# A graph layer's tail: neighbour sums scaled by diagonal matrices on TensorE instead of per-row factors on ScalarE and VectorE

## The reference, cut to what matters

```python
agg = segment_sum(alpha[:, None] * z[edge_src], edge_dst)   # alpha = e_exp / denom[edge_dst]
h_new = h_s + agg                                           # h_s = xn @ W_self.T
h_new = where(deg[:, None] > 0, h_new, h)                   # h = xn; a node without edges keeps its row
h_new = relu(h_new)
x = x + (xn + h_new) + mix(xn)
y = layernorm(x)                                            # goes to the router and the experts
```

## Time and profile before

| | us |
|---|---|
| median of 3 executions | 2349.81 (2349.37 to 2350.4) |
| the profiled execution's own time | 2345.32 |
| its span, first to last instruction | 2343.3 |
| busy in the span: PE / DVE / ACT / POOL | 1930.4 / 1649.2 / 687.6 / 1465.6 |
| mean granted TensorE clock | 0.879 |

### The profile page before, as it was taken

One profiled execution on the slowest core, in us unless ns is written; L12 is line 12 of the kernel. 1 busy time (PEld: TensorE's weight loads), 2 busy tenths in 40 slices (PEclk: granted clock), 3 DMA queues, 4 the chain that ended last, 5 costly groups with the idle time before them and its releaser, 6 DMA issues.

```text
span 2343.3 us, 43283 instructions
## 1 busy us (share of the span) xinstructions
PE 1930.4 (82%) x11471; PEld 1505.6 (64%) x11471; DVE 1649.2 (70%) x4135; ACT 687.6 (29%) x2860; POOL 1465.6 (63%) x1188
## 2 busy tenths in 40 slices
PE   6999699678888888888888888888867778899991
PEld 5555688556666666666666656666644458788881
DVE  6997699977777767777666766776756656445564
ACT  2444688531111111111111111111102344444550
POOL 5000556677888888888888788888780153744366
PEclk9999555579899999998898988889998789999996
DMA  8887888544445544445544444445557754545464
GB/s 216 260 256 226 280 284 295 160 126 121 123 123 132 154 124 124 123 125 146 138 123 122 124 123 122 122 123 138 138 124 182 171 154 113 154 136 145 138 171 124
DMA packets 308206, 368.12 MB, mean 157 GB/s; under 512 B 118624, under 2 KB 261707, under 8 KB 304982
## 3 DMA queue, kind: packets, MB, share of 16 engines
q1 hardware_dynamic: 165292, 223.65, 32.0%
q0 software_dynamic: 135840, 136.92, 24.4%
q10 hardware_dynamic: 6975, 6.40, 0.9%
HBM read 279.68 MB, written 85.98 MB: 156 GB/s over the span
## 4 chain that ended last, share of the span: by engine, by line
PE 40%; issue 13%; DVE 11%; DMA 7%; DVEq 4%; POOL 3%; SPq 2%; ACT 1%; ACTq 0%; POOLq 0%
PE bank L677 39%; DMA wexp<-func_rows,a_src 5%; DVE acc L1823 4%; DVEq L1580 2%; POOL wexp L641 2%; DVE onehot L1810 1%; DMA g_all<-sorted_d 1%; SPq L369 1%; POOL g_all L664 1%; PE bank L1026 1%; DVE work L1596 1%; DVEq L1823 1%; DVE work L1599 1%; DMA work<-mix_rows 0%; PE bank L849 0%
## 5 line engine op out<-in xcount | busy, mean ns | idle before, releaser
L641 POOL DMA_INDIRECT wexp<-func_rows,a_src x850 | 1060.9, 1248 | 263.4 <-issue 193.7
L677 PE MATMUL bank<-wexp,onehot 125*125 125x257 f32 x1700 | 557.2, 432 | 215.6 <-DVE acc L1823 156.1
L1823 DVE TENSOR_TENSOR acc<-bank,acc 125x257 f32 x850 | 355.7, 419 | 381.0 <-PE bank L677 244.4
L677 PEld LDWEIGHTS bank<-wexp,onehot 125*125 125x125 f32 x1700 | 316.8, 206 | 391.9 <-issue 298.2
L1810 DVE TENSOR_SCALAR onehot<-iota_r,a_rel,a_hi 125x125 f32<-125x125 f32 x850 | 320.7, 380 | 0.1
L609 POOL TENSOR_TENSOR work<-iota_h,a_hi 125x500 f32<-125x500 f32 x85 | 109.2, 1286 | 246.9 <-PE bank L714 165.4
L677 PE MATMUL bank<-g_all 128*128 128x128 f32 x1840 | 230.0, 278 | 15.4 <-issue 6.1
L654 POOL DMA_INDIRECT sorted_d<-acc,work x100 | 122.4, 1224 | 180.9 <-DVE acc L1967 98.0
L677 PEld LDWEIGHTS bank<-g_all 128*128 128x128 f32 x1840 | 217.8, 194 | 19.0 <-ACT g_all L1301 7.4
L664 POOL DMA_INDIRECT g_all<-y_d,work x100 | 131.0, 1310 | 139.2 <-DVE g_all L2137 77.8
L677 PE MATMUL bank<-w_s,work 128*125 128x256 f32 x800 | 216.2, 419 | 0.0
(11 more groups left out here) (275 smaller groups left out, 2817.4 us busy)
## 6 DMA issues: line engine op xcount, KB each, us to landing
wexp<-lr_d SPq DMA_DIRECT2D x85, 625.0 KB
wexp<-in_attr SPq DMA_DIRECT2D x25, 896.0 KB
sorted_d<-spare SPq DMA_DIRECT2D x72, 256.0 KB, 4.8
g_all<-sorted_d SPq DMA_DIRECT2D x115, 128.0 KB
y_d<-g_all SPq DMA_DIRECT2D x115, 128.0 KB, 3.1
wexp<-func_rows,a_src POOLq DMA_INDIRECT x850, 4.0
work<-xn_rows SPq DMA_DIRECT2D x38, 224.0 KB
xnT_d<-work SPq DMA_DIRECT2D x25, 250.0 KB, 4.4
```

The source lines that it names most:

```text
L641: pool.indirect_dma_start(ring[:, z, 0:D], None, func_rows, bass.IndirectOffsetOnAxis(ap=a_src[:, n // CS, n % CS:n % CS + 1], axis=0)).th ...
L677: return pe.matmul(o, l, r, start=first, stop=last_, **kw)
L1823: v.tensor_tensor(to, bank[3 + z % 2][0:R, 0:D + 1], to, ALU.add).then_inc(s("summed"), 1)
```

## The change: diagonal matrices and four products

ScalarE no longer touches the self rows. For each group it writes four matrices of 125x125 into a new buffer `diag` (two buffers, in slots of `g_all` that hold expert outputs later): the identity with its rows scaled by `have` for either block, and by `rden` for either block. TensorE multiplies the self rows by the first and the accumulator by the second, per block, into the same PSUM region: four calls of 256 columns in place of two of 512. `xn` is no longer part of it. VectorE then adds `xn` to the PSUM result in one instruction of 125x512, in place of the two of 125x256. All four products now wait for the group's four diagonals; these wait for `rden` (semaphore `have` at 3) and for the buffer, not for the group's loads.

```diff
+        diag = [g_all[0:R, 11 + k].rearrange("p j n -> p (j n)")[:, 0:4 * R].rearrange("p (a n) -> p a n", a=4) for k in range(2)]
...
                 freed(pe, s("c_r"), 2 * (g - 1))
                 pe.wait_ge(s(f"group_in{k}"), 32 * GIN[k] + 96 * (g // CBUF + 1))
                 to = pr_(2 + 2 * (g % 2))
-                mm(to, ident[0:R, 0:R], c_xn[k], True, False)
-                pe.wait_ge(s("c_have"), 2 * g + 2)
-                mm(to, ident[0:R, 0:R], c_self[k], False, True).then_inc(s("c_gnn"), 1)
+                pe.wait_ge(s("c_have"), 4 * g + 4)
+                for j in range(2):
+                    mm(to[:, j], diag[g % 2][:, j], c_self[k][:, j], True, False)
+                    last = mm(to[:, j], diag[g % 2][:, 2 + j], accv[:, 2 * g + j, 0:D], False, True)
+                last.then_inc(s("c_gnn"), 1)
...
-            def have_self(g):
-                k = g % CBUF
-                act.wait_ge(s("have"), 1)
-                act.wait_ge(s(f"group_in{k}"), 32 * GIN[k] + 96 * (g // CBUF + 1))
-                for j in range(2):
-                    act.activation(c_self[k][:, j], c_self[k][:, j], ACT.Copy,
-                                   scale=have[:, 2 * g + j:2 * g + j + 1]).then_inc(s("c_have"), 1)
+            def diagonals(g):
+                act.wait_ge(s("have"), 3)
+                freed(act, s("c_gnn"), g - 1)
+                for a, to_ in enumerate((have, rden)):
+                    for j in range(2):
+                        act.activation(diag[g % 2][:, 2 * a + j], ident[0:R, 0:R], ACT.Copy,
+                                       scale=to_[:, 2 * g + j:2 * g + j + 1]).then_inc(s("c_have"), 1)
...
-            o.did(v.reciprocal(rden, rden))
+            v.reciprocal(rden, rden).then_inc(s("have"), 1)
             v.wait_ge(s("have"), 1)
 
             def rows(g):
 
                 k = g % 2
                 v.wait_ge(s("c_gnn"), g + 1)
-                if g == 0:
-                    o.settle()
-                for j in range(2):
-                    v.scalar_tensor_tensor(c_x1[k][:, j], accv[:, 2 * g + j, 0:D], rden[:, 2 * g + j:2 * g + j + 1],
-                                           pr_(2 + 2 * k)[:, j], ALU.mult, ALU.add).then_inc(s("c_r"), 1)
+                v.wait_ge(s(f"group_in{g % CBUF}"), 32 * GIN[g % CBUF] + 96 * (g // CBUF + 1))
+                v.tensor_tensor(c_x1[k], pr_(2 + 2 * k), c_xn[g % CBUF], ALU.add).then_inc(s("c_r"), 2)
                 v.wait_ge(s("c_r"), 2 * g + 2)
                 v.sem_inc(s("c_t"), 1)
-                v.wait_ge(s(f"group_in{g % CBUF}"), 32 * GIN[g % CBUF] + 96 * (g // CBUF + 1))
```

More of the change, by code:

```diff
@@ L1276, in _ @@
                 if i < GROUPS:
-                    have_self(i)
+                    diagonals(i)
                 if 0 <= i - 1 < GROUPS:
```

## The result

| | before | after |
|---|---|---|
| median of 10 runs each, us | 2345.06 (2334.15 to 2350.4) | 2354.36 (2346.56 to 2362.56) |
| profiled execution, its own time and span, us | 2345.32, 2343.3 | 2351.19, 2349.1 |
| mean granted TensorE clock | 0.879 | 0.883 |

The ratio is 1.0043, 95% interval 1.0026 to 1.006: about 10.1 us slower (6.1 to 14.1); the two medians are 9.3 apart. The forecast was +9.8 us, set on the three runs known then, whose median of 2349.81 is 4.75 above that of the ten; so 2359.6 is 5.2 above what was measured, and the difference is nearly that of the forecast. By the same shift of the base 2354.36 lies just under the 2355 to 2367 that the forecast gave for itself. How much of that is luck, the stage has to show.

What follows compares the result with a forecast made beforehand. DMA was taken to bound groups up to 1847 us, a ring of waits (4.265 us a turn) those from 1860. Ring, routing and end terms of 7.8 plus 2.0 at the start gave +9.8, 2359.6 us, range 2353.5 to 2368.

Steps and rivals of the forecast that it cites:

- The ring that is late next: Diagonals, products, transposes, router, router_relu, next diagonals in one iteration: 4.91 us a turn, overtaking the old ring's 4.76.
- Groups 13 to 24: Behind the routing: nine turns at 0.65 us more, 5.8, plus 0.14 at the first and 0.85 behind the last.
- the clock rival: TensorE's longer stands lower its clock repeatedly, 3.0 us more per slow turn; six give +28, 2378 us; chance 0.11.
- Before the routing: Group 13's diagonals and products stand ahead of the logits it needs: 0.32 + 0.85 = 1.2 us.
- The start and the DMA-bound groups: Group 0's rows and the loads they release come 2.5 us later, shifting landings +2.0; full DMA hides the longer ring.
- if the DMA engines were not full: In the groups taken as DMA-bound, 8 more turns would cost 0.65 us each, 5.2.
- VectorE and the end: One add of 125x512 takes 0.683 us in place of 0.87; VectorE's step at the end is 0.18 shorter.
- The sum: Over the whole kernel: 7.8 + 2.0 = +9.8 us, 2359.6 us for the median.
- Partly hidden: Diagonals ready during ScalarE's waits, start lost in DMA backlog: only +2 to +4 us, 2352 to 2354; chance 0.12.
- VectorE binds: Products and diagonals fit under VectorE's round, each turn 0.18 us shorter if the new ring is under 3.87; chance 0.04.
- The signs: Proof of error: turns under 4.3 us, a first row before 1783, or clock well under 0.97 behind 1860 us.

Runs made afterwards that it cites:

- e3: The kernel before with ScalarE's two activations on the self rows made four of half the size; turns behind the routing averaged 4.57 us.
- e2: The kernel before with TensorE's wait for the scaled self rows moved ahead of both identity products; turns from group 15 to 24 averaged 4.74 us.
- e5: The changed kernel run again with no edit; its stage took 153.20 us, as in its first profile.
- e9: The changed kernel with one load of expert weights per group in place of two, for twice as many groups; ratio 1.0031.
- e1: The kernel before run again with no edit; its stage took 141.33 us, against 142.54 in its first profile.
- e6: The kernel before with one load of expert weights per group in place of two, for twice as many groups; ratio 0.9971.
- e4: The changed kernel with the diagonals made three groups ahead, in four buffers; ratio 1.0018.
- e11: The changed kernel with the diagonals made three groups ahead and one load of expert weights per group in place of two; ratio 0.9949.
- e8: The kernel before with ScalarE scaling the self rows one group ahead; ratio 1.0003.
- e7: The changed kernel with diagonals three groups ahead and all of GpSimd's sends held back until the last group is normalized; 2401.09 us.

## Why the prediction was right, step by step

**The ring that is late next.** Right. The forecast was a turn of 4.91, and it is 5.04 to 5.05 on average, in three executions. By terms, forecast against the turn shown above: diagonals 1.22 and 1.26; semaphore to TensorE 0.06 and 0.14; products 1.81 and 1.81 (the forecast's own two terms, 1.76 and 0.1, add up to 1.86, so 1.81 to the hundredth is partly luck); transposes 0.42 and 0.42; router 1.05 and 1.05; router_relu to diagonals 0.35 and 0.37. The semaphore is the largest miss. The 0.06 was read where the first product had run before the wait, and e3 has it so too (1890.10 to 1890.15); where all products stand behind the wait it is 0.14, here and in e2 (1887.95 to 1888.09). e2 came out above its forecast as well, 4.74 against 4.69. The Trainium skill's page "ScalarE: Activation LUTs" (What ACT_TABLE_LOAD costs) gave an estimated 1.25 for the four activations; the trace agrees with it, 1.25 to 1.26, more closely than with my 1.22.

**Groups 13 to 24.** Forecast +6.8 (5.8, 0.14 and 0.85), measured +8.76 against the one profile of before and +9.58 against the other. The nine turns from group 15 to group 24 cost 6.9 where 5.8 was forecast, 0.77 each in place of 0.65, about the 0.14 by which the turn was set too short. The two turns before them cost 1.8 where the other terms gave 1.0, and the larger part of that is one turn, group 14 to 15, at the slow clock:

```profile
1864.59 0.68 DVE L1950 TENSOR_TENSOR work<-bank,g_all 125x512 f32<-125x512 f32 x1
...
1872.08 0.68 DVE L1950 TENSOR_TENSOR work<-bank,g_all 125x512 f32<-125x512 f32 x1
```

```profile
1866.00:1870.00 4.00, 4.00 (x13) 3.15 (x13) 1.12 (x5) 0.72 (x3) 3.33 (x3) 0.50 0.92 257
```

It takes 7.49 us (7.52 and 7.53 in e5 and e9, 7.48 in e2), where the two profiles of before have 5.97 and 4.59. The granted clock is 0.50, 1.2 GHz, from the routing up to 1870 us, and each of its products is recorded with 1.06 in place of 0.59. In the first profile of before it had returned to 1.00 between 1860 and 1866 and fell only behind that, as in e2; in e1 it was slow without a break, as here, but full again about 4 us sooner, counted from group 13's rows. The forecast left this spell as it was. In the four executions in which TensorE has no product left to do during ScalarE's work, the turn is 7.5 us; why was not tried. So the clock rival was right in that the slow clock costs more here, once: this turn is 1.5 us longer than in the first profile of before and 2.9 longer than in e1, where the ring alone gives 0.77. Its own mechanism, further spells through the longer stand in every turn, did not occur: TensorE stood 1.47 us per turn (about 1.3 forecast), and behind the spell the clock is full:

```profile
1870.00:1875.00 5.00, 3.53 (x20) 3.07 (x19) 3.11 (x9) 2.27 (x7) 3.82 (x4) 0.96 0.62 177
1875.00:1880.00 5.00, 3.53 (x22) 3.10 (x21) 3.10 (x9) 2.63 (x9) 4.06 (x3) 1.00 0.81 234
```

**Before the routing.** Forecast 1.2 us; 12 to 13 is +0.95, or -2.0 against e1, whose 19.40 has loads in it.

**The start and the DMA-bound groups.** The size came near, for a wrong reason. Group 0's rows were forecast 2.5 us later and are 2.77. The DMA share of the first window is indeed lower (0.92, from 1.04), but no later turn waits for a load; the delay of the start is passed on through the turns instead. From the start to group 4 it is +5.25 us, and I had costed those turns at nothing. VectorE's first three turns are no longer than before (3.87, 3.86 and 4.12, from 4.05, 4.04 and 4.03); all of the 2.48 us shows in the fourth, 8.03 from 5.28, where VectorE first waits for logits (1.76 us in the kernel before):

```profile
1801.39 0.17 DVE L1973 TENSOR_TENSOR work<-bank,rb_bc 125x12 f32<-125x12 f32 x1 [4.69 <-PE bank L678]
```

There the longer products and diagonals of the turns so far, part of them at the slow clock, are paid at once. The step that failed is "a group of 1.28 MB at 223 GB/s lands every 5.7 us, more than 4.91, so the longer ring is hidden there". 223 GB/s is the mean of a window, 1800 to 1847 us, and not a pace at which groups land: after takes one group in 5.05 us in even turns, e2 one in 4.72. With the ring at 5.05 us the late loads are gone, and in the net groups 4 to 12 are 4.33 us shorter than in the first profile of before and 0.4 shorter than in e1. So up to group 12 the sum was forecast at +2.0 and came out at +0.9 and +4.6: the ring's full price, less what the loads gave back. That it lies near +2.0 is luck. The prediction's other figure, 5.2 us "if the DMA engines were not full", is 6.3 by e6 and e9.

**VectorE and the end.** The one add of 125x512 takes 0.68 as forecast. The end was forecast 0.18 shorter and is 0.03 longer (0.29 shorter than in e1), too small to judge.

**The sum** was 9.8; the stage shows 10.66 and 11.87, the ratio 10.1. *Partly hidden* (0.12) is refuted by the turns: none of the addition is hidden behind VectorE. *VectorE binds* (0.04) is refuted for this kernel, but its number was right: once e4 took the diagonals off the ring, VectorE's round was 3.85 to 3.88, and the rival had named 3.87.

**The signs.** Of what would have shown the prediction wrong, none of the turns behind the routing was under 4.3 (the least is 4.73). The first row did come before 1783, at 1782.24, but only because the loop ended 2.76 us earlier in this execution: counted from the loop's end it is 2.77 later. The clock is 0.93 in the window from 1863 us, under 0.97, by the one spell above.

## What to carry to other kernels

Work that moves from one engine to another is priced on the ring it lands on: here the vector work saved was 0.18 us a turn, while the product that used to run during ScalarE's activations, put behind its semaphore, cost 0.47. When operands depend on nothing in the ring, make them a few groups ahead before judging the idea: with spread loads in both, that took the changed kernel from 1.0031 (e9) to 0.9949 (e11). And a full DMA share is not a pace. Before hiding work behind "DMA-bound" groups, halve the loads per group or slow the consumer once, and see whether the pace is the loads' own.

## What was not expected of the hardware

**A DMA share above 1 with and without late loads.** Over groups 4 to 12, e5 has a share of 1.09 and 234 GB/s with turns of 5.04 to 5.05, e2 1.12 and 248 GB/s with turns of 4.67 to 4.78, and the kernel before 1.12 and 231 GB/s with turns of 4.03 to 7.66. Neither the share nor the rate says which of them waits; the evenness of the turns does. That loads which pile up are served more slowly is not shown: e1 waits at 237 GB/s, and after does not at 229.

**TensorE's results can come late beside GpSimd's indirect sends.** In e4, behind the routing, the semaphore increments of the last products, the transposes, the router and the logits land as follows (their times in the trace, us):

```
products 1884.85   transposes 1885.61   router 1886.37   logits 1887.87
products 1890.14   transposes 1890.89   router 1892.38   logits 1893.16
```

Such steps, of 0.71 to 0.77 and 1.48 to 1.58 us, are in e8 as well. In e4 they are 0.75 us or whole multiples of it (0.76, 0.76, 1.50, 2.27, 0.75, 1.49, 0.78), and two of them are the distance between two sends, 1.50 us:

```profile
1884.10 1.19 POOL L655 DMA_INDIRECT sorted_d<-acc,work  x1 [0.31 <-issue]
1885.60 1.19 POOL L655 DMA_INDIRECT sorted_d<-acc,work  x1 [0.30 <-issue]
1887.09 1.19 POOL L655 DMA_INDIRECT sorted_d<-acc,work  x1 [0.30 <-issue]
```

In e7, without sends, the same four land at 1888.92, 1889.76, 1890.61 and 1890.94, steps of 0.84, 0.85 and 0.33, which fit the recorded products. The recorded ends are modelled and do not show the delay: in e4 the last product of that group is recorded from 1882.0 to 1882.6, and its increment comes at 1884.85. Neither before nor after shows it in its steady turns, though GpSimd sends there too, and e11 has whole turns of 3.85 beside sends. In e11's longest turn, 6.29, the increments come with the recorded ends, so that turn has another cause, which was not traced. So the delay was seen only beside sends, and sends are not enough for it; what else it takes stays open, and no run here tries it.
